# Mixture layers: the gate and up products of a tile as seven block products (Strassen) in place of eight, interleaved with the down products

## Chip, core and metric

The kernel runs on one core of a Trainium2 chip. The metric is the device time of one execution in microseconds (us); lower is better. The core has a matrix engine (PE, TensorE, with its weight loads shown as PEld), three engines for elementwise work (DVE or VectorE, ACT or ScalarE, POOL or GpSimd), and SyncE (SP), which here issues DMAs. Engines run their own instruction streams in order and wait for each other by semaphores.

## What is computed

Four layers, each an attention and a feed-forward, on 1024 tokens of width 256. The change touches the three mixture-of-experts feed-forwards (layers 1, 2 and 3). Cut to what matters, such a layer is

```
comb   = router weights per token and expert (top 2 of 8, 8 of 32, 4 of 16)
routed = sum over experts e of  comb[:, e] * ((silu(x @ w_gate[e]) * (x @ w_up[e])) @ w_down[e])
shared = (silu(x @ sw_gate) * (x @ sw_up)) @ sw_down        (layer 3: times a sigmoid gate)
x      = x + routed + shared
```

All experts are computed for all tokens, and the coefficient of a token that did not choose an expert is 0.

## The kernel before

**Tiles.** The hidden columns of the shared expert and of all experts are laid side by side and cut into tiles of 128: 14 tiles in layer 1, 34 in layer 2, 28 in layer 3, 76 in all (NT is a layer's number). A tile is one weight block of 128 hidden units against all 1024 tokens, which are held transposed (width on the partitions, two blocks k of 128; tokens in two halves c of 512).

**Three passes.** Every float32 operand of the big products is split into a rounded high part and the rest (type fp32r), and a product is three matmuls: high x high, high x low, low x high. So gate of one half is 2 blocks k times 3 passes, 6 matmuls of 128x128 by 128x512; up is 6 more; both halves make 24. The down product of a half is 2 output blocks times 3 passes, 6 matmuls, 12 for the tile. A tile is 36 matmuls.

**PSUM.** Eight banks of 128x512: p_g0, p_g1 (gate), p_u0, p_u1 (up) and the four p_y, in which the down products of all tiles add up.

**Work of the other engines on a tile.** ACT rounds the weights (`up_hi`, `down_hi`), takes the silu of the gate (`act_g`) and rounds the hidden values (`hid_hi`, by `high`). POOL makes the low parts of the weights (`up_lo`, `down_lo`) and multiplies by the coefficients (`hid`, by `weigh`). DVE multiplies silu by up (`gated`, by `gate`) and makes `hid_lo` (by `low`). SP loads weights and, for each routed tile, coefficient rows spread over partitions.

**Order.** There is no scheduler: each engine's order is written by hand in `mixture`, as a loop of two tiles (`Step` gives a loop-dependent tile number, `wait` a loop-dependent semaphore value). On PE it is gate and up of tile t+1, then down of tile t:

```
                        gate_up(Step(g, r + 2, 2))
                        down(Step(g, r + 1, 2))
```

On DVE it is `gate(t, 0)`, `gate(t, 1)`, `low(t, 0)`, `low(t, 1)`; on POOL `split_up(t + 1)`, `weigh(t, 0)`, `weigh(t, 1)`, `split_down(t + 1)`. Ahead of the loop each layer has a head: a layer norm, the transposes of x (`x_t`, split into `x_hi` and `x_lo`), the router on DVE, and tiles 0 and 1 written out, whose gate and up products PE runs while DVE ranks the experts.

## Time and profile before

| | before |
|---|---|
| median of 3 runs | 1289.76 us (1284.64 to 1299.0) |
| profiled execution: span, first to last instruction | 1274.6 us |
| PE busy | 1100.8 us, 86% |
| DVE busy | 674.0 us, 53% |
| ACT busy | 640.8 us, 50% |
| POOL busy | 524.5 us, 41% |
| granted TensorE clock, mean | 0.929 of full |

The times of single instructions below come from the one profiled execution, whose time is known as its span of 1274.6 us; the median of the runs is 15.2 us above that span. A row of the timeline reads: start, duration, engine, line, operation, output<-inputs, shapes, and in brackets how long the engine was idle before it and what released it. Matmuls of 512 columns start 0.23 us apart in a steady stretch while each is shown as 0.39 us long, since they overlap in the array; so the distance of starts, not the duration, is what a matmul costs.

### The profile page before, as it was taken

Reading aid. Unit: us, or ns where it says so; the run is one execution under the profiler, and the core shown is the slowest. Engines: PE = TensorE matmul, PEld = TensorE weight load, DVE = VectorE, ACT = ScalarE, POOL = GpSimd, SP = SyncE. Lnnn points to the kernel's source line nnn. Section 1 sums busy time; section 2 is a strip of 40 time slices with the busy share of each in tenths; the row PEclk is TensorE's granted clock in tenths of the full one; section 3 lists DMA queues with packets and bytes.
Section 4 is the critical chain, followed back from the end, with each engine's and each line's share of the span. In section 5 each row is a group of like instructions: output and inputs, shape, how many; then the busy total and the mean of one; then the engine's idle time right before and its main releaser. Section 6 shows DMA issues by size and latency. Waiting matters only on the chain. (4 is left out here: it accounts for less than half of the span.)

```text
span 1274.6 us, 19803 instructions
## 1 busy us (share of the span) xinstructions
PE 1100.8 (86%) x6973; PEld 799.6 (63%) x6974; DVE 674.0 (53%) x1388; ACT 640.8 (50%) x1016; POOL 524.5 (41%) x587
## 2 busy tenths in 40 slices
PE   4999622699699978998799999999967699999998
PEld 3545311444388865554578888888633478888887
DVE  5768578631653347785753333333577873333333
ACT  4557558489543334776334334443283454334443
POOL 5145700001246632123256656666401035666664
PEclk8789966899899998999799999999989889999999
DMA  5863130368223305431133353333100014333332
GB/s 162 244 191 125 52 115 1 84 181 193 77 96 115 112 29 160 147 116 46 53 120 115 115 177 110 111 111 106 37 9 1 1 40 145 115 113 107 111 110 69
DMA packets 65942, 131.40 MB, mean 103 GB/s; under 512 B 9307, under 2 KB 33051, under 8 KB 65366
## 3 DMA queue, kind: packets, MB, share of 16 engines
q1 hardware_dynamic: 62470, 123.10, 32.1%
q10 hardware_dynamic: 3120, 5.64, 1.4%
q0 software_dynamic: 288, 1.84, 0.4%
q8 instruction: 37, 0.61, 0.2%
q14 instruction: 27, 0.22, 0.1%
HBM read 114.51 MB, written 15.45 MB: 102 GB/s over the span
## 5 line engine op out<-in xcount | busy, mean ns | idle before, releaser
L1506 POOL TENSOR_TENSOR f_hid<-f_gated,f_coef 128x512 f32<-128x512 f32 x152 | 220.6, 1453 | 166.6 <-DVE f_gated L1538 157.0
L1538 DVE TENSOR_TENSOR f_gated<-f_act_g,f_p_u 128x512 f32<-128x512 f32 x152 | 104.2, 687 | 262.2 <-PE f_p_u L1322 245.6
L828 ACT ACTIVATE a_probs<-a_p_sc 128x1024 f32<-128x1024 f32 x192 | 188.9, 1020 | 27.4 <-PE a_p_sc L730 19.6
L1434 ACT ACTIVATE f_hid_hi<-f_hid 128x512 fp32r<-128x512 f32 x152 | 96.2, 633 | 203.8 <-POOL f_hid L1506 203.8
L959 DVE TENSOR_REDUCE a_maxes<-a_p_max 128x2 f32<-128x512 f32 x256 | 160.0, 682 | 41.6 <-PE a_p_max L697 41.4
L1542 DVE TENSOR_TENSOR f_hid_lo<-f_hid,f_hid_hi 128x512 fp32r<-128x512 f32 x152 | 112.6, 741 | 127.8 <-ACT f_hid_hi L1434 126.5
L1429 ACT ACTIVATE f_act_g<-f_p_g 128x512 f32<-128x512 f32 x152 | 90.4, 597 | 152.7 <-PE f_p_g L1322 148.5
L730 PE MATMUL a_p_sc<-a_q,a_k 75*128 75x256 bf16 (+1 forms) x768 | 117.8, 282 | 9.8 <-ACT a_probs L828 5.1
L1335 PE MATMUL f_p_y<-f_hid_hi,f_down_hi 128*128 128x512 f32 x292 | 114.0, 390 | 0.0
L1335 PE MATMUL f_p_y<-f_hid_hi,f_down_lo 128*128 128x512 f32 x292 | 113.7, 389 | 0.0
L1335 PE MATMUL f_p_y<-f_hid_lo,f_down_hi 128*128 128x512 f32 x292 | 113.7, 389 | 0.0
L750 PE MATMUL a_p_out<-a_probs,all_v 128*32 128x256 f32 x1536 | 110.7, 403 | 1.2 <-ACT a_probs L828 1.2
L1493 POOL TENSOR_TENSOR f_up_lo<-f_w,f_up_hi 128x512 fp32r<-128x512 f32 x76 | 97.6, 1285 | 31.4 <-DVE all_xn L183 20.1
L730 PEld LDWEIGHTS a_p_sc<-a_q,a_k 75*128 75x128 bf16 (+1 forms) x768 | 69.0, 100 | 56.4 <-issue 22.1
L697 PE MATMUL a_p_max<-a_k,a_q 72*128 72x256 bf16 x512 | 91.9, 293 | 12.3 <-DMA a_q<-q_parts 6.3
L1493 POOL TENSOR_TENSOR f_down_lo<-f_w,f_down_hi 128x256 fp32r<-128x256 f32 x76 | 70.5, 927 | 76.7 <-ACT f_down_hi L1424 76.7
L1322 PE MATMUL f_p_g<-f_x_hi,f_up_hi 128*128 128x512 f32 x304 | 95.8, 397 | 0.0
L1322 PE MATMUL f_p_g<-f_x_hi,f_up_lo 128*128 128x512 f32 x304 | 95.0, 394 | 0.0
L1322 PE MATMUL f_p_g<-f_x_lo,f_up_hi 128*128 128x512 f32 x304 | 94.9, 394 | 0.0
L1322 PE MATMUL f_p_u<-f_x_hi,f_up_hi 128*128 128x512 f32 x304 | 94.6, 392 | 0.0
L1322 PE MATMUL f_p_u<-f_x_lo,f_up_hi 128*128 128x512 f32 x304 | 93.9, 391 | 0.0
L1322 PE MATMUL f_p_u<-f_x_hi,f_up_lo 128*128 128x512 f32 x304 | 93.7, 389 | 0.0
(309 smaller groups left out, 1706.5 us busy)
## 6 DMA issues: line engine op xcount, KB each, us to landing
f_w<-in_w SPq DMA_DIRECT2D x76, 384.0 KB, 3.5
f_coef<-coef SPq DMA_DIRECT2D x49, 512.0 KB, 3.7
a_q<-q_parts SPq DMA_DIRECT2D x48, 288.0 KB
a_k<-k_plain SPq DMA_DIRECT2D x96, 96.0 KB
outs<-a_out SPq DMA_DIRECT2D x48, 128.0 KB, 1.7
a_whole<-outs SPq DMA_DIRECT2D x48, 128.0 KB, 2.6
q_parts<-a_q_part SPq DMA_DIRECT2D x48, 96.0 KB, 3.6
a_k<-k_unit SPq DMA_DIRECT2D x24, 192.0 KB
```

The lines of the kernel that those rows point to most:

```text
L697: last = nc.tensor.matmul(p_max[:, n % 3, t * D:(t + 1) * D], q_of(b, h, ROWS)[:, t * P:(t + 1) * P], k_of(b, h, ROWS), start=True, stop=True)
L730: last = nc.tensor.matmul(p_sc[pair % 2][:, h % 2, t * D:(t + 1) * D], k_of(b, h, K_ROWS)[:, t * P:(t + 1) * P], q_of(b, h, K_ROWS), start ...
L750: last = nc.tensor.matmul(p_out[32 * j:32 * j + 32, 0:D], m.v[:, b, at:at + 32], probs[b % 2][:, h, t, :], start=(quarter == 0), stop=(qua ...
L828: nc.scalar.activation(probs[b % 2][:, 2 * pair:2 * pair + 2, :, :].rearrange("p h t d -> p h (t d)"), p_sc[pair % 2][:], ACT.Exp, scale=s ...
L959: nc.vector.tensor_reduce(maxes[b % 3][:, :, h], p_max[:, n % 3, :].rearrange("p (t d) -> p t d", t=NK), axis=AX.X, op=ALU.max, negate=Tru ...
L1322: last = nc.tensor.matmul(p[:], w_[n][:, (2 * k + s) * P:(2 * k + s + 1) * P], x_[:, k, tok], start=(i == 0), stop=(i == len(passes) - 1))
L1335: last = nc.tensor.matmul(p_y[o][c][:], w_[n][:, o * P:(o + 1) * P], h_[n][c][:], start=False, stop=stop and i == len(passes) - 1, skip_gr ...
L1434: nc.scalar.activation(hid_hi[slot(t, 2)][c][:], hid[c][:], ACT.Copy).then_inc(hid_hi_done, 1)
L1493: nc.gpsimd.tensor_tensor(lo[slot(t, 2)][:], w[slot(t, 2)][:, cols], hi[slot(t, 2)][:], ALU.subtract).then_inc(lo_ready, 1)
L1506: nc.gpsimd.tensor_tensor(hid[c][:], gated[c][:], coef[slot(t, 2)][:, c * 512:(c + 1) * 512], ALU.mult).then_inc(hid_done, 1)
L1538: nc.vector.tensor_tensor(gated[c][:], act_g[c][:], p_u[c][:], ALU.mult).then_inc(gated_done, 1)
L1542: nc.vector.tensor_tensor(hid_lo[slot(t, 2)][c][:], hid[c][:], hid_hi[slot(t, 2)][c][:], ALU.subtract).then_inc(hid_lo_done, 1)
```

## The change

Gate and up of a tile are seen as one product of a 2x2 block matrix of weights (rows gate and up, columns the two width blocks k: A11, A12, A21, A22) with a 2x2 block matrix of tokens (rows k, columns the token halves: X11, X12, X21, X22). In place of eight block products (24 matmuls) it is made of seven, M1 to M7 (21 matmuls), in the Winograd form of Strassen's algorithm. What that adds:

- per tile, on DVE, `sum_weights`: four 128x128 sums of weight blocks, as one instruction of 3x128 and one of 2x128 columns, all in SBUF, for two tiles ahead;
- per tile, the split into high and low parts is 1024 columns wide in place of 512 (ACT `split_up`, POOL `split_up`);
- per tile, three copies of a PSUM bank to SBUF on ACT (`copy_m7`, `copy_m1`, `copy_u2`) and three adds of such a copy to a PSUM bank on DVE (`add_c11`, `add_c21`, `add_c22`), since an intermediate product goes into more than one result;
- once per layer, four sums of token blocks of 512 columns (`x_sum`) with their splits, ahead of the router's work on DVE and ahead of the first `weigh` on POOL;
- the four banks of gate and up become p_a0, p_a1 (by turns), p_b and p_cc, so one tile's products are no longer each in a bank of their own;
- weights come in two transfers per tile (up and down parts apart); the up part of tile t+2 is loaded once POOL has made `up_lo` of tile t.

Tiles 0 and 1 keep the eight products. From tile 2 on, all orders are new: the down products of tile t-1 lie between the block products of tile t, and `weigh`, `high` and `low` of the second half of tile t-1 lie in tile t. The diff, cut to its core (new semaphores, the heads and the second list of the last tile left out; `last_tile` is `tile` with m3 one step earlier):

```diff
@@ -1161,6 +1161,10 @@
 MIXTURES = {1: Mixture(8, 2, 176, 352), 2: Mixture(32, 8, 128, 256), 3: Mixture(16, 4, 176, 704)}
 GROUPS, TOP_GROUPS, ROUTED_SCALE = 8, 4, 2.5
 UP = NK * 2 * P
+SUMS = 2 * UP
+GATE_AT, UP_AT = (0, 3), (1, 2)
+A11, A21, A22, A12, S3, R2, S1, S4, V = range(9)
+X11, X12, X21, X22, T1, P2, T3, P4 = range(8)
...
-        x_hi = st.sb("x_hi", [P, NK, T], F32R)
-        x_lo = st.sb("x_lo", [P, NK, T], F32R)
+        x_hi = st.sb("x_hi", [P, 4 * NK, 512], F32R)
+        x_lo = st.sb("x_lo", [P, 4 * NK, 512], F32R)
...
+        x_sum = m.xn[:].rearrange("p (b i) d -> p b (i d)", b=4)
+        m1_copy, m7_copy, u2_copy = x_t[:, 0, 0:512], x_t[:, 0, 512:1024], x_t[:, 1, 0:512]
...
-        w = [st.sb(f"w{n}", [P, UP + D]) for n in range(2)]
-        up_hi = [st.sb(f"up_hi{n}", [P, UP], F32R) for n in range(2)]
-        up_lo = [st.sb(f"up_lo{n}", [P, UP], F32R) for n in range(2)]
+        w_up = [st.sb(f"w_up{n}", [P, SUMS + P]) for n in range(2)]
+        w_down = [st.sb(f"w_down{n}", [P, D]) for n in range(2)]
+        up_hi = [st.sb(f"up_hi{n}", [P, SUMS], F32R) for n in range(2)]
+        up_lo = [st.sb(f"up_lo{n}", [P, SUMS], F32R) for n in range(2)]
...
+        p_a, p_b, p_cc = p_g, p_u[1], p_u[0]
...
+                def load_up(t):
+                    if t >= 2:
+                        sp.wait_ge(up_lo_ready, t - 1)
+                    sp.dma_start(w_up[t % 2][:, 0:UP], a[f"w{layer}"][t, :, 0:UP]).then_inc(up_loaded[t % 2], 16)
+                def load_down(t):
+                    if t >= 2:
+                        sp.wait_ge(down_lo_ready, t - 1)
+                    sp.dma_start(w_down[t % 2][:], a[f"w{layer}"][t, :, UP:UP + D]).then_inc(down_loaded[t % 2], 16)
...
-                    if t > 2:
-                        wait(sp, down_lo_ready, t, 1, -1)
-                        sp.dma_start(w[t % 2][:], a[f"w{layer}"][t, :, :]).then_inc(w_loaded[t % 2], 16)
+                    load_down(t)
...
+                    if t + 2 < NT:
+                        load_up(t + 2)
...
+                def product(t, bank, w_at, x_at, start, done):
                     n = slot(t, 2)
+                    for i, (w_, x_) in enumerate(((up_hi, x_hi), (up_hi, x_lo), (up_lo, x_hi))):
+                        last = nc.tensor.matmul(bank[:], w_[n][:, w_at * P:(w_at + 1) * P], x_[:, x_at, :],
+                                                start=start and i == 0, stop=(i == 2), skip_group_check=True)
+                    last.then_inc(done, 1)
+                def m7(t):
+                    wait(pe, up_lo_ready, t, 1, 1)
+                    wait(pe, gated_done, t, 2, -1)
+                    product(t, p_cc, S3, T3, True, m7_done)
+                def m1(t):
+                    wait(pe, silu_done, t, 2, -2)
+                    product(t, p_a[slot(t, 2)], A11, X11, True, m1_done)
+                def m2(t):
+                    wait(pe, gated_done, t, 2, 0)
+                    product(t, p_b, A12, X21, True, m2_done)
+                def m6(t):
+                    wait(pe, m1_copied, t, 1, -1)
+                    product(t, p_a[slot(t, 2)], R2, P2, False, m6_done)
+                def m4(t):
+                    wait(pe, m7_copied, t, 1, -1)
+                    product(t, p_cc, A22, P4, False, m4_done)
+                def m5(t):
+                    wait(pe, u2_copied, t, 1, -1)
+                    product(t, p_a[slot(t, 2)], S1, T1, False, m5_done)
+                def m3(t):
+                    wait(pe, c22_done, t, 1, -1)
+                    product(t, p_a[slot(t, 2)], S4, X22, False, m3_done)
...
+                def tile(t):
+                    m7(t)
+                    m1(t)
+                    down(t + (-1), 0, 0)
+                    m2(t)
+                    m6(t)
+                    m4(t)
+                    down(t + (-1), 0, 1)
+                    m5(t)
+                    down(t + (-1), 1, 0)
+                    down(t + (-1), 1, 1)
+                    m3(t)
...
-                        gate_up(Step(g, r + 2, 2))
-                        down(Step(g, r + 1, 2))
-                down(NT - 1, stop=True)
+                        tile(Step(g, r + 2, 2))
+                tile(NT - 2)
+                last_tile(NT - 1)
+                for c in range(2):
...
+                def split_up(t, width=SUMS):
+                    if width == SUMS:
+                        wait(act, summed, t, 1, -1)
+                    else:
+                        act.wait_ge(up_loaded[t], 16)
+                    nc.scalar.activation(up_hi[slot(t, 2)][:, 0:width], w_up[slot(t, 2)][:, 0:width],
                                          ACT.Copy).then_inc(up_hi_ready, 1)
...
+                def silu_first(t):
+                    wait(act, c11_done, t, 1, -1)
+                    nc.scalar.activation(act_g[0][:], p_b[:], ACT.Silu).then_inc(silu_done, 1)
+                def silu_second(t):
+                    wait(act, m3_done, t, 1, -1)
+                    nc.scalar.activation(act_g[1][:], p_a[slot(t, 2)][:], ACT.Silu, scale=-1.0).then_inc(silu_done, 1)
+                def copy_m1(t):
+                    wait(act, m1_done, t, 1, -1)
+                    nc.scalar.activation(m1_copy, p_a[slot(t, 2)][:], ACT.Copy).then_inc(m1_copied, 1)
+                def copy_m7(t):
+                    wait(act, m7_done, t, 1, -1)
+                    nc.scalar.activation(m7_copy, p_cc[:], ACT.Copy).then_inc(m7_copied, 1)
+                def copy_u2(t):
+                    wait(act, m6_done, t, 1, -1)
+                    nc.scalar.activation(u2_copy, p_a[slot(t, 2)][:], ACT.Copy).then_inc(u2_copied, 1)
...
+                    copy_m7(t)
+                    copy_m1(t)
                     if more:
                         split_up(t + 1)
-                    silu(t, 0)
-                    silu(t, 1)
+                    high(t + (-1), 1)
+                    copy_u2(t)
+                    silu_first(t)
+                    split_down(t)
                     high(t, 0)
-                    high(t, 1)
-                    if more:
-                        split_down(t + 1)
+                    silu_second(t)
...
+                def split_up(t, width=SUMS):
+                    wait(pool, up_hi_ready, t, 1, 1)
+                    nc.gpsimd.tensor_tensor(up_lo[slot(t, 2)][:, 0:width], w_up[slot(t, 2)][:, 0:width],
+                                            up_hi[slot(t, 2)][:, 0:width], ALU.subtract).then_inc(up_lo_ready, 1)
...
+                    weigh(t + (-1), 1)
                     if more:
                         split_up(t + 1)
                     weigh(t, 0)
-                    weigh(t, 1)
-                    if more:
-                        split_down(t + 1)
+                    split_down(t)
...
+                def sum_weights(t):
+                    tile_w = w_up[slot(t, 2)]
+                    dve.wait_ge(up_loaded[slot(t, 2)], uses(t, 2) * 16 + 16)
+                    nc.vector.tensor_tensor(blocks(tile_w, S3, 2, 3), blocks(tile_w, A11, 1, 3),
+                                            blocks(tile_w, A21, 1, 3), ALU.subtract).then_inc(differed, 1)
+                    wait(dve, differed, t, 1, -1)
+                    nc.vector.tensor_tensor(blocks(tile_w, R2, 2, 2), blocks(tile_w, S3, 0, 2),
+                                            blocks(tile_w, A22, V - A22, 2), ALU.add).then_inc(summed, 1)
+                def add_c11(t):
+                    wait(dve, m2_done, t, 1, -1)
+                    wait(dve, m1_copied, t, 1, -1)
+                    nc.vector.tensor_tensor(p_b[:], p_b[:], m1_copy, ALU.add).then_inc(c11_done, 1)
+                def add_c21(t):
+                    wait(dve, m4_done, t, 1, -1)
+                    wait(dve, u2_copied, t, 1, -1)
+                    nc.vector.tensor_tensor(p_cc[:], p_cc[:], u2_copy, ALU.add).then_inc(c21_done, 1)
+                def add_c22(t):
+                    wait(dve, m5_done, t, 1, -1)
+                    wait(dve, m7_copied, t, 1, -1)
+                    nc.vector.tensor_tensor(p_b[:], p_a[slot(t, 2)][:], m7_copy, ALU.add).then_inc(c22_done, 1)
+                def gate_first(t):
+                    wait(dve, silu_done, t, 2, 1)
+                    wait(dve, c21_done, t, 1, -1)
+                    nc.vector.tensor_tensor(gated[0][:], act_g[0][:], p_cc[:], ALU.mult).then_inc(gated_done, 1)
+                def gate_second(t):
+                    wait(dve, silu_done, t, 2, 2)
+                    wait(dve, c22_done, t, 1, -1)
+                    nc.vector.scalar_tensor_tensor(gated[1][:], p_b[:], -1.0, act_g[1][:], ALU.mult,
+                                                   ALU.mult).then_inc(gated_done, 1)
...
+                def tile(t, more=True):
+                    if more:
+                        sum_weights(t + 2)
+                    add_c11(t)
+                    low(t + (-1), 1)
+                    add_c21(t)
+                    gate_first(t)
+                    add_c22(t)
                     low(t, 0)
-                    low(t, 1)
+                    gate_second(t)
...
+                x11, x12, x21, x22 = [x_t[:, k, c * 512:(c + 1) * 512] for k in range(NK) for c in range(2)]
+                v.scalar_tensor_tensor(x_sum[:, 0, :], x11, -1.0, x12, ALU.mult, ALU.subtract).then_inc(x_sum_ready, 1)
+                dve.wait_ge(x_sum_ready, 1)
+                v.tensor_tensor(x_sum[:, 1, :], x_sum[:, 0, :], x22, ALU.subtract).then_inc(x_sum_ready, 1)
+                v.tensor_tensor(x_sum[:, 2, :], x22, x12, ALU.add).then_inc(x_sum_ready, 1)
+                dve.wait_ge(x_sum_ready, 2)
+                v.tensor_tensor(x_sum[:, 3, :], x21, x_sum[:, 1, :], ALU.subtract).then_inc(x_sum_ready, 1)
+                sum_weights(2)
...
-    gu = gu.reshape(2, NK, P, mx.tiles, P).transpose(3, 2, 1, 0, 4).reshape(mx.tiles, P, UP)
+    gu = gu.reshape(2, NK, P, mx.tiles, P)
+    gu = np.stack([gu[0, 0], gu[1, 0], gu[1, 1], gu[0, 1]], 0).transpose(2, 1, 0, 3).reshape(mx.tiles, P, UP)
```

DVE, the loop body for one tile in layer 1, before (f1_gated0 is half 0, f1_hid_lo10 the low part of slot 1, half 0):

```order
L1538 TENSOR_TENSOR f1_gated0<-f1_act_g0,f1_p_u0 128x512
L104 REGISTER_ALU
L1538 TENSOR_TENSOR f1_gated1<-f1_act_g1,f1_p_u1 128x512
L1542 TENSOR_TENSOR f1_hid_lo10<-f1_hid0,f1_hid_hi10 128x512
L1542 TENSOR_TENSOR f1_hid_lo11<-f1_hid1,f1_hid_hi11 128x512
```

The same engine and place now (f1_w_up0 holds the weight blocks and their sums, f1_x_t the three copies):

```order
L1698 TENSOR_TENSOR f1_w_up0<-f1_w_up0 128x3x128
L104 ISA
L1701 TENSOR_TENSOR f1_w_up0<-f1_w_up0 128x2x128
L104 REGISTER_ALU
L1707 TENSOR_TENSOR f1_p_u1<-f1_p_u1,f1_x_t 128x512
L104 ISA
L1732 TENSOR_TENSOR f1_hid_lo11<-f1_hid1,f1_hid_hi11 128x512
L1712 TENSOR_TENSOR f1_p_u0<-f1_p_u0,f1_x_t 128x512
L104 REGISTER_ALU
L1722 TENSOR_TENSOR f1_gated0<-f1_act_g0,f1_p_u0 128x512
L1717 TENSOR_TENSOR f1_p_u1<-f1_p_g0,f1_x_t 128x512
L1732 TENSOR_TENSOR f1_hid_lo00<-f1_hid0,f1_hid_hi00 128x512
```

Four instructions per tile have become nine (the ninth, gate_second, follows the last row). The two sums come first, and the low part of the other half of the tile before stands between two adds on which later products wait.

POOL, one tile of the loop in layer 1, before:

```order
L1493 TENSOR_TENSOR f1_up_lo0<-f1_w0,f1_up_hi0 128x512
L1504 ISA
L104 ISA
L1506 TENSOR_TENSOR f1_hid0<-f1_gated0,f1_coef1 128x512
L104 REGISTER_ALU
L1506 TENSOR_TENSOR f1_hid1<-f1_gated1,f1_coef1 128x512
L1493 TENSOR_TENSOR f1_down_lo0<-f1_w0,f1_down_hi0 128x256
```

And now:

```order
L1656 TENSOR_TENSOR f1_hid1<-f1_gated1,f1_coef1 128x512
L104 ISA
L1638 TENSOR_TENSOR f1_up_lo1<-f1_w_up1,f1_up_hi1 128x1024
L1654 ISA
L104 REGISTER_ALU
L1656 TENSOR_TENSOR f1_hid0<-f1_gated0,f1_coef0 128x512
L104 REGISTER_ALU
L1643 TENSOR_TENSOR f1_down_lo0<-f1_w_down0,f1_down_hi0 128x256
```

The low part of the up weights is twice as wide and stands between the two halves' multiplications by coefficients, right behind the second half of the tile before.

## Rows read from the trace of the kernel before

**Rows 1.** The page: first line, part 1, and the first of part 4's lines:

```profile
span 1274.6 us, 19803 instructions
PE 1100.8 (86%) x6973; PEld 799.6 (63%) x6974; DVE 674.0 (53%) x1388; ACT 640.8 (50%) x1016; POOL 524.5 (41%) x587
PE f_p_g L1322 6%; PE f_p_u L1322 6%; PE f_p_y L1335 6%; PE f_p_y L1371 0%; DVE f_ln_stats L152 0%; PE f_p_y L1348 0%; DVE all_xn L183 0%; DVE all_x L1634 0%; PE f_p_y L1381 0%; DVE f_x_t L1562 0%; PE f_p_y L1392 0%; DVE f_y_t L1631 0%; DVE f_ln_mv L159 0%; DVEq L1269 0%; ACT f_ln_root L139 0%
```

**Rows 2.** Windows: stretch, length, each engine's busy time, granted clock, DMA share, GB/s:

```profile
1100.00:1116.32 16.32, 16.32 (x74) 13.52 (x73) 5.34 (x9) 6.58 (x12) 10.31 (x8) 1.00 0.37 112
627.60:630.00 2.40, 2.40 (x8) 1.92 (x8) 1.50 (x5) 1.67 (x2) 0.00 (x0) 0.50 0.01 3
```

**Rows 3.** Timeline of one tile of layer 3, in the loop:

```profile
1101.98 0.62 PE L1322 MATMUL f_p_g<-f_x_hi,f_up_hi 128*128 128x512 f32 x2
...
1105.61 0.62 PE L1322 MATMUL f_p_g<-f_x_hi,f_up_lo 128*128 128x512 f32 x2
1105.74 1.29 POOL L1506 TENSOR_TENSOR f_hid<-f_gated,f_coef 128x512 f32<-128x512 f32 x1 [0.53 <-DVE f_gated L1538]
...
1106.27 0.60 ACT L1429 ACTIVATE f_act_g<-f_p_g 128x512 f32<-128x512 f32 x1 [2.12 <-PE f_p_g L1322]
...
1107.07 0.63 ACT L1434 ACTIVATE f_hid_hi<-f_hid 128x512 fp32r<-128x512 f32 x1 [0.20 <-POOL f_hid L1506]
...
1107.69 0.69 DVE L1538 TENSOR_TENSOR f_gated<-f_act_g,f_p_u 128x512 f32<-128x512 f32 x1 [2.03 <-PE f_p_u L1322]
...
1108.30 0.68 DVE L1542 TENSOR_TENSOR f_hid_lo<-f_hid,f_hid_hi 128x512 fp32r<-128x512 f32 x1
...
1108.46 1.68 POOL L1506 TENSOR_TENSOR f_hid<-f_gated,f_coef 128x512 f32<-128x512 f32 x1 [1.43 <-DVE f_gated L1538]
...
1110.14 0.62 PE L1322 MATMUL f_p_g<-f_x_hi,f_up_hi 128*128 128x512 f32 x2
```

**Rows 4.** Timeline, DVE and POOL at once, layer 1:

```profile
360.23 1.29 POOL L1506 TENSOR_TENSOR f_hid<-f_gated,f_coef 128x512 f32<-128x512 f32 x1 [1.39 <-DVE f_gated L1538]
360.33 1.73 DVE L1542 TENSOR_TENSOR f_hid_lo<-f_hid,f_hid_hi 128x512 fp32r<-128x512 f32 x1
...
363.46 1.29 POOL L1493 TENSOR_TENSOR f_up_lo<-f_w,f_up_hi 128x512 fp32r<-128x512 f32 x1
...
364.02 0.67 DVE L1538 TENSOR_TENSOR f_gated<-f_act_g,f_p_u 128x512 f32<-128x512 f32 x1
```

**Rows 5.** Timeline, layer 2: POOL's two rows, then DVE's:

```profile
639.34 0.74 POOL L1493 TENSOR_TENSOR f_down_lo<-f_w,f_down_hi 128x256 fp32r<-128x256 f32 x1 [1.05 <-ACT f_down_hi L1424]
640.04 1.46 POOL L1493 TENSOR_TENSOR f_up_lo<-f_w,f_up_hi 128x512 fp32r<-128x512 f32 x1
...
639.46 0.91 DVE L1612 TENSOR_TENSOR f_picked<-f_picked,f_scores 128x256 f32<-128x256 f32 x1
```

**Rows 6.** Groups of instructions: count, busy us, mean ns, idle before:

```profile
L1424 ACT ACTIVATE f_down_hi<-f_w 128x256 fp32r<-128x256 f32 x76 | 30.5, 401 | 0.0
L2271 DVE TENSOR_TENSOR c_s<-c_s,c_top 128x1024 f32<-128x1024 f32 x8 | 9.8, 1225 | 0.3
L1855 ACT ACTIVATE b_junk<-b_h 128x1024 f32<-128x1024 f32 x8 | 8.5, 1060 | 0.1
```

**Rows 7.** Timeline, head of layer 2:

```profile
628.66 1.06 PE L1322 MATMUL f_p_g<-f_x_lo,f_up_hi 128*128 128x512 f32 x2
629.52 1.05 PE L1322 MATMUL f_p_g<-f_x_hi,f_up_lo 128*128 128x512 f32 x2
...
642.18 1.06 PE L1392 MATMUL f_p_y<-all_ident,f_by_token 128*33 128x128 f32 x8 [1.40 <-DVE f_by_token L1619]
```

**Rows 8.** Timeline, end of layer 3:

```profile
1265.88 0.69 DVE L1542 TENSOR_TENSOR f_hid_lo<-f_hid,f_hid_hi 128x512 fp32r<-128x512 f32 x1 [1.85 <-ACT f_hid_hi L1434]
...
1266.62 0.50 PE L1335 MATMUL f_p_y<-f_hid_hi,f_down_hi 128*128 128x512 f32 x1
```

**Rows 9.** DMA issues: KB each, median us to landing:

```profile
f_w<-in_w SPq DMA_DIRECT2D x76, 384.0 KB, 3.5
```

184 lines of the change are left out of this document (119 added, 65 removed).

## The prediction

> **What bounds the kernel now.** I read the page's first part and the chain that ended last, then a stretch inside a mixture loop by windows, then one tile of the timeline, and at last the places where DVE and POOL work at once. PE is busy 86% of the span and heads the chain, with gate, up and down at about equal shares [rows 1]. In a 16.32 us stretch of layer 3 PE is busy all of it at clock 1.00, while POOL is busy 10.31 us, ACT 6.58 and DVE 5.34 [rows 2]. The first gate matmul of one tile starts at 1101.98 and that of the next at 1110.14 [rows 3]: a period of 8.16 us for 36 matmuls, 0.2267 us each, with nothing idle. So the loop is bound by the number of matmuls, and everything else is hidden as long as it keeps up. The loop rows repeat in all three layers; of the 76 tiles, NT - 3 periods per layer lie between the start of tile 2 and that of the last tile: 11 + 31 + 25 = 67.
>
> **What is taken away.** 3 of 36 matmuls per tile: 3 x 0.2267 = 0.68 us. If PE stays the bound, the period is 33 x 0.2267 = 7.48 us, and 67 periods give 45.6 us.
>
> **What is added, and whether it is hidden.** By busy time all engines still fit. ACT: three 512-wide copies at 0.60 (taken as the silu's row), the split at 1.06 (the 1024-wide row) in place of 0.6, the rest as before (two silus at 0.60, two highs at 0.63, 0.40 for down): 5.7 us [rows 3, 6]. DVE: gates and adds read one operand from PSUM, 5 x 0.69; two lows at 0.68; the sums of 3x128 and 2x128 columns at 0.56 and 0.43, from the 0.68 of 512 and the 1.225 of 1024 columns: 5.8 us [rows 3, 6]. POOL: 512 columns take 1.29 us, 256 take 0.74, so 1024 take about 2.39; with two weighs and the down part 5.7 us [rows 3, 5]. On that count alone PE would be late for nothing.
>
> But DVE and POOL shut each other out. At 360.33 DVE starts a low part 0.10 us behind a POOL multiplication that ends at 361.52; DVE ends at 362.06, after 1.73 us in place of 0.68 [rows 4]: it got through only 0.54 us after POOL was done. The other way round, POOL's weigh at 1108.46 meets a low part that ends at 1108.98 and ends itself at 1110.14: 1.68 us, 1.16 of them after the low part [rows 3]. An instruction of DVE that reads two operands in SBUF and one of POOL thus take turns. A gate, which reads one from PSUM, doesn't: it takes 0.67 us in the middle of POOL's work [rows 4]. And who asks first gets in first: between two POOL instructions back to back, at 640.08, a waiting DVE instruction of 256 columns gets in, ends 0.29 us later, and the second POOL one takes 1.46 [rows 5]. Before, this costs nothing, since DVE waits most of the time.
>
> The change puts five kinds of such work in one narrow place. Time in which the pair is held, per tile: POOL 1.16 + 1.16 for the weighs, 0.60 for the down part (0.74 less the 0.13 that POOL needs ahead of it), and for the 1024-wide low part 1.16 + 2 x 0.55 = 2.26; DVE 0.54 + 0.54 for the lows, 0.42 and 0.29 for the sums. Sum 6.97 of 7.48 us. The pair would have to be held without a break, but what it does is chained.
>
> **The chain of one tile,** from the start of gate_second of tile t-1 (0) to that of tile t, each step by the rows above: DVE issues the sum of three blocks 0.61 later (the distance from 1107.69 to 1108.30 [rows 3]), asks 0.14 later, and holds for 0.42: 1.17. The weigh of tile t-1's second half asked meanwhile, holds 1.16: 2.33. The sum of two blocks has asked by then, holds 0.29: 2.62. POOL's 1024-wide low part is next in its queue and holds 2.26: 4.88. All this while DVE has done c11 and stands at low(t-1, 1), whose input (ACT's high) has been ready since about 3.0 but which asked after POOL: it ends 0.54 later, 5.42. Behind it in DVE's queue are add_c21 (issued 0.08 before that end, 0.69, and 0.03 to the wait for its own result) to 6.06 and gate_first to 6.75. Then POOL weighs half 0 (0.05 + 1.29) to 8.09, ACT rounds it (0.04 + 0.63) to 8.76, DVE starts low(t, 0) at 8.80 and gate_second 0.61 later: 9.41 us per tile. PE finds low(t-1, 1) missing for the down products of half 1 (some 1.2 us idle), and c22 missing for m3 (some 0.6). 7.48 + 1.9 is the same 9.4.
>
> So each period grows by 9.41 - 8.16 = 1.25 us: 67 x 1.25 = +84 us, where PE alone would have given -46.
>
> Bounds of this term. The one row that doesn't exist is the 1024-wide POOL instruction. If it let DVE in halfway, as two of 512 would by [rows 5], DVE's low part would come 1.1 us earlier and the loop close at 8.3 us: +9 us. If the sum of three blocks loses its turn against the weigh (it asks only 0.12 us earlier), it and the second sum come behind longer POOL work and the loop closes at about 10.0: +123 us. The adds, which write PSUM, have no row either; between 0.6 and 1.0 us they move the period to 9.3 and 9.7. I take 9.41, since every hold that is shown lasted to the end of its instruction. The Trainium skill (page SBUF — State Buffer, section Who interferes with whom) calls this an exclusive lock: a VectorE instruction with two SBUF inputs and a GpSimd one that reads SBUF block each other for the full instruction. Taken to the letter it would also hold for the 0.13 and 0.14 us at the start of each, which the rows show outside the lock; the sum by it would be some 0.5 us more per tile.
>
> **Heads and ends.** Four sums of 512 columns and the first weight sums stand ahead of the router's chain on DVE: 4 x 0.61 + 1.0 = 3.5 us, more where POOL is in the way. In layer 2 PE already waits 1.40 us for that chain [rows 7], so all of it is late there, in the other two I count 3 to 4: +4 us each, +12 (between 0 and 24). At the end of a layer PE waited little before: the last low part ended at 1266.57 and PE went on at 1266.62 with 12 matmuls before it to hide it [rows 8]. Now gate_second of the last tile follows m3, and only one down block and half 0 lie beside silu 0.60, gate 0.69, weigh 1.29, high 0.63, low 0.69: +2.5 each, +7.
>
> **Cover that holds.** Weights of tile t+2 are asked for when up_lo of tile t is done, some 5 us before DVE's sums need them; such a load took 3.5 us at 1.5 times the size [rows 9]. If it took over 5 us, the sums, and with them all of DVE, would wait for it.
>
> **The sum.** 84 + 12 + 7 = +103 on the span of 1274.6: 1378. The median of the runs is 15.2 above the span before; kept, that is 1289.8 + 103 = 1393 us.
>
> **Rivals.**
> 1. *PE stays the bound* (faster). The pair of DVE and POOL finds its gaps in another order than I have laid out, and the period is 7.48. For it: all busy times fit. Against: [rows 3, 4, 5], and 6.97 of 7.48 us held. -46 + 12 + 7 = -27: 1263 us. It decides if the long POOL instruction doesn't shut DVE out.
> 2. *The long low part shuts DVE out only in part.* Period 8.3 to 8.9: +9 to +50, with heads and ends 1318 to 1359 us.
> 3. *Sum and weigh change places.* Period 10.0: 1289.8 + 123 + 19 = 1432 us. They ask 0.12 us apart, so it could also come and go.
> 4. *The clock falls.* In the head of layer 2 the granted clock is 0.50 [rows 2] and pairs of matmuls start 0.86 us apart in place of 0.45 [rows 7], 1.2 against 2.4 GHz. PE would then need 33 x 0.43 = 14.2 us per tile. With idle times of at most 1.2 us in a tile I think it stays at 1.00; if a tenth of the loop ran so, that is some 7 tiles times 4.8 us, +34 us on the forecast.
> 5. *It doesn't do what it says*: 21 matmuls in place of 24 stand in the order, so this is excluded.
>
> **Chances.** Forecast (1365 to 1420) 0.66; rival 1 0.12, of which 0.01 within 1%; rival 2 0.11; rival 3 0.07; rival 4 0.04. Less than 1% can't be told from no change by such measurements. Faster by over 1% 0.12, within 1% 0.03, slower 0.85. The range leaves out rival 1 and the lower half of rival 2 and takes in nearly all else: 1330 to 1435.
>
> **What the profile after would show.** Starts of the second silu 9.4 us apart in all three loops. In rows of DVE: f_hid_lo at a mean of 1.3 us or more, half of them over 2 us and each of these ending half a microsecond after the 1024-wide f_up_lo, which takes 2.4 to 2.6; the two-block sum at 1.4 and not 0.43. DVE busy about 89% of a stretch, PE's idle time in front of f_p_y, released by f_hid_lo, and in front of m3, released by DVE's add. Granted clock 1.00. I am wrong if f_hid_lo keeps its 0.69 us beside the long POOL instruction, or if PE is idle for a reason other than these two.

## The result: 8.8% slower

The changed kernel takes 1401.74 us (median of 4 runs, 1399.15 to 1406.09), the kernel before 1289.11 (4 runs, 1284.64 to 1299.0): ratio 1.0877, 95% interval 1.0822 to 1.0932. Forecast were 1393 us and a range of 1330 to 1435.

The page of the changed kernel, its first line, part 1 and the first two lines of part 4 (the chain that ended last); [rows 1] answers to it:

```profile
span 1404.3 us, 20549 instructions
...
PE 1125.2 (80%) x6763; PEld 755.1 (54%) x6764; DVE 1032.7 (74%) x1750; ACT 773.2 (55%) x1238; POOL 604.0 (43%) x599
...
issue 9%; POOL 9%; DVE 2%; DMA 1%; ACT 1%; POOLq 0%; PE 0%; DVEq 0%; SPq 0%
POOL f_up_lo L1638 4%; POOL f_hid L1656 3%; POOL f_down_lo L1643 1%; POOL f_x_lo L1649 0%; DMA coef<-f_coef_t 0%; DMA f_coef<-coef 0%; ACT f_hid_hi L1567 0%; DVE f_x_lo L1762 0%; DVE f_ln_stats L152 0%; DVE all_xn L183 0%; DVE f_x_t L1757 0%; PE f_p_y L1413 0%; DVE all_x L1844 0%; POOLq L104 0%; DVE f_p_u L1712 0%
```

PE has 210 matmuls fewer and yet 24 us more of busy time. About 9 us of that lie in the three loops, where its rows grow when it restarts after a pause; 8 lie in the heads, where the lower granted clock lasts longer in layers 1 and 2, and 8 ahead of the first mixture, in code that is the same. The chain is now led by POOL, with the long low part of the up weights first in it. One window of one period in layer 3 (columns as in [rows 2]):

```profile
1198.00:1207.46 9.46, 8.24 (x34) 5.91 (x33) 7.87 (x10) 5.07 (x9) 6.06 (x5) 1.00 0.30 97
```

No engine is busy all of it (DVE 83%, PE 87%), and the granted clock is 1.00: this loop is bound by an order of turns, not by an engine's work. Behind the loops' entries the starts of the second `gate` lie 9.45 to 9.48 us apart in all three layers, where before a period was 8.16 [rows 3]. That shows in the groups of instructions (count, busy us, mean ns, idle before and its releaser):

```profile
L1732 DVE TENSOR_TENSOR f_hid_lo<-f_hid,f_hid_hi 128x512 fp32r<-128x512 f32 x152 | 206.9, 1362 | 118.5 <-ACT f_hid_hi L1567 118.3
...
L1638 POOL TENSOR_TENSOR f_up_lo<-f_w_up,f_up_hi 128x1024 fp32r<-128x1024 f32 (+1 forms) x76 | 186.3, 2451 | 27.2 <-DVE all_xn L183 20.1
...
L1413 PE MATMUL f_p_y<-f_hid_hi,f_down_hi 128*128 128x512 f32 x292 | 128.3, 440 | 71.4 <-DVE f_hid_lo L1732 71.4
L1372 PE MATMUL f_p_g<-f_x_hi,f_up_hi 128*128 128x512 f32 x280 | 117.6, 420 | 23.5 <-DVE f_p_u L1717 23.5
...
L1701 DVE TENSOR_TENSOR f_w_up<-f_w_up 128x256 f32<-128x256 f32 x70 | 93.5, 1336 | 2.4
```

`f_hid_lo` takes 1.36 us on average and not 0.69, the two-block sum 1.34 and not 0.43. Nearly all of PE's idle time in the loops stands in front of the two products named: 71.4 us ahead of the down products, released by `f_hid_lo`, and 23.5 us ahead of m3, released by DVE's add. The timeline of that tile:

```profile
1202.65 0.69 DVE L1717 TENSOR_TENSOR f_p_u<-f_p_g,f_x_t 128x512 f32<-128x512 f32 x1
...
1203.40 0.50 PE L1372 MATMUL f_p_g<-f_x_hi,f_up_hi 128*128 128x512 f32 x1 [0.34 <-DVE f_p_u L1717]
...
1205.40 0.69 DVE L1727 SCALAR_TENSOR_TENSOR f_gated<-f_p_u,f_act_g 128x512 f32<-128x512 f32 x1
...
1206.00 0.55 DVE L1698 TENSOR_TENSOR f_w_up<-f_w_up 128x384 f32<-128x384 f32 x1
1206.17 1.54 POOL L1656 TENSOR_TENSOR f_hid<-f_gated,f_coef 128x512 f32<-128x512 f32 x1 [1.37 <-DVE f_gated L1727]
...
1206.59 1.41 DVE L1701 TENSOR_TENSOR f_w_up<-f_w_up 128x256 f32<-128x256 f32 x1
...
1207.67 2.58 POOL L1638 TENSOR_TENSOR f_up_lo<-f_w_up,f_up_hi 128x1024 fp32r<-128x1024 f32 x1
...
1207.92 0.69 DVE L1707 TENSOR_TENSOR f_p_u<-f_p_u,f_x_t 128x512 f32<-128x512 f32 x1
...
1208.52 2.29 DVE L1732 TENSOR_TENSOR f_hid_lo<-f_hid,f_hid_hi 128x512 fp32r<-128x512 f32 x1
...
1210.73 0.69 DVE L1712 TENSOR_TENSOR f_p_u<-f_p_u,f_x_t 128x512 f32<-128x512 f32 x1
...
1210.86 0.50 PE L1413 MATMUL f_p_y<-f_hid_hi,f_down_hi 128*128 128x512 f32 x1 [0.86 <-DVE f_hid_lo L1732]
```

The low part that starts at 1208.52 ends at 1210.81, 0.56 us after POOL's wide instruction (1210.25), as behind the short one in [rows 4]; each of the 64 low parts of over 2 us in the trace ends 0.54 or 0.55 us after one (by unrounded times). The add at 1207.92, with an operand in PSUM, takes its 0.69 in the middle of it.

**Where the time went.** Of each profiled execution I took the stretch from a layer's first low part of the up weights to its last add on x: before 125.5, 292.1 and 241.6 us in layers 1 to 3, after 148.5, 343.7 and 288.7, +122 in all.
- Heads, to the start of tile 2: before 21.4, 24.6, 23.2, after 26.0, 31.6, 28.1: +16.5. Four of the runs below (e2, e3, e7, e9) leave these heads' work as it is and take 30.4 in layer 2; in the changed kernel the granted clock fell to 0.50 for 3.4 us at the end of that head, which is about the difference.
- Periods: 67 x 1.30 = +87.
- Entry to the loop: the second and third periods are longer than 9.46 by 1.6, 2.9 and 7.3 in the three layers: +11.7. Part of it is the clock (see e9).
- Ends: what is left of the difference, about +6.

Outside the mixtures the span is 7.9 us longer, 6.9 of it ahead of the first one, in code that the change leaves alone; this point also moved between the other kernels (347 to 359 us), so I don't count it to the change.

### The profile page after: what moved, and what is told of

Its sections match the earlier page's. It is cut to its first block and busy times, and to the rows that moved or that the text cites. A ratio compares the mean times of both kernels' runs of the same rounds, so it can differ in the third digit from the quotient of the medians.

```text
span 1404.3 us, 20549 instructions
## 1 busy us (share of the span) xinstructions
PE 1125.2 (80%) x6763; PEld 755.1 (54%) x6764; DVE 1032.7 (74%) x1750; ACT 773.2 (55%) x1238; POOL 604.0 (43%) x599
## 5 line engine op out<-in xcount | busy, mean ns | idle before, releaser
L1732 DVE TENSOR_TENSOR f_hid_lo<-f_hid,f_hid_hi 128x512 fp32r<-128x512 f32 x152 | 206.9, 1362 | 118.5 <-ACT f_hid_hi L1567 118.3
L1638 POOL TENSOR_TENSOR f_up_lo<-f_w_up,f_up_hi 128x1024 fp32r<-128x1024 f32 (+1 forms) x76 | 186.3, 2451 | 27.2 <-DVE all_xn L183 20.1
L1413 PE MATMUL f_p_y<-f_hid_hi,f_down_hi 128*128 128x512 f32 x292 | 128.3, 440 | 71.4 <-DVE f_hid_lo L1732 71.4
L1372 PE MATMUL f_p_g<-f_x_hi,f_up_hi 128*128 128x512 f32 x280 | 117.6, 420 | 23.5 <-DVE f_p_u L1717 23.5
L1413 PEld LDWEIGHTS f_p_y<-f_hid_hi,f_down_hi 128*128 128x128 f32 x292 | 55.0, 188 | 126.3 <-DVE f_hid_lo L1732 108.6
L1372 PE MATMUL f_p_g<-f_x_lo,f_up_hi 128*128 128x512 f32 x280 | 110.2, 394 | 0.0
L1372 PE MATMUL f_p_g<-f_x_hi,f_up_lo 128*128 128x512 f32 x280 | 110.1, 393 | 0.0
L969 DVE RECIPROCAL a_inv<-a_whole 128x64 f32<-128x64 f32 (+1 forms) x48 | 45.5, 947 | 81.0 <-DMA a_whole<-outs 81.0
L1701 DVE TENSOR_TENSOR f_w_up<-f_w_up 128x256 f32<-128x256 f32 x70 | 93.5, 1336 | 2.4
L1372 PEld LDWEIGHTS f_p_g<-f_x_hi,f_up_hi 128*128 128x128 f32 x280 | 52.8, 189 | 63.2 <-DVE f_p_u L1717 53.1
```

The costliest lines, as they stand in the source:

```text
L1372: last = nc.tensor.matmul(bank[:], w_[n][:, w_at * P:(w_at + 1) * P], x_[:, x_at, :], start=start and i == 0, stop=(i == 2), skip_group_ch ...
L1413: last = nc.tensor.matmul(p_y[o][c][:], w_[n][:, o * P:(o + 1) * P], h_[n][c][:], start=False, stop=stop and i == len(passes) - 1, skip_gr ...
L1638: nc.gpsimd.tensor_tensor(up_lo[slot(t, 2)][:, 0:width], w_up[slot(t, 2)][:, 0:width], up_hi[slot(t, 2)][:, 0:width], ALU.subtract).then_i ...
L1701: nc.vector.tensor_tensor(blocks(tile_w, R2, 2, 2), blocks(tile_w, S3, 0, 2), blocks(tile_w, A22, V - A22, 2), ALU.add).then_inc(summed, 1)
L1732: nc.vector.tensor_tensor(hid_lo[slot(t, 2)][c][:], hid[c][:], hid_hi[slot(t, 2)][c][:], ALU.subtract).then_inc(hid_lo_done, 1)
```

## The experiments

The first four ran with 13 runs of the kernel before (median 1290.84), the next four with 7 (1292.01), the last with 11 (1289.68). "Period" is the distance between starts of the second gate.

| run | median us (range) | ratio to before, 95% | period |
|---|---|---|---|
| changed kernel | 1401.74 (1399.15–1406.09) | 1.0877 (1.0822–1.0932) | 9.46 |
| e1_two_halves | 1334.73 (1331.21–1335.84) | 1.0344 (1.0289–1.0399) | 8.36 |
| e2_low_later | 1364.91 (1360.95–1366.83) | 1.0565 (1.0506–1.0623) | 8.73 |
| e3_no_sums | 1373.83 (1372.2–1379.53) | 1.0640 (1.0583–1.0697) | 9.04 |
| e4_pool_writes_only | 1299.99 (1292.14–1306.22) | 1.0090 (1.0053–1.0126) | 7.86 |
| e5_before_21 | 1238.57 (1234.01–1241.21) | 0.9603 (0.9573–0.9633) | 7.48 |
| e6_no_input_sums | 1395.98 (1392.29–1400.72) | 1.0828 (1.0791–1.0865) | 9.46 |
| e7_reorder | 1310.69 (1309.66–1314.05) | 1.0161 (1.0127–1.0195) | 7.96 |
| e8_reorder_head | 1308.07 (1304.12–1309.52) | 1.0139 (1.0108–1.0169) | 7.96 |
| e9_load_early | 1398.38 (1396.91–1400.88) | 1.0839 (1.0803–1.0875) | 9.46 |

**e1: the wide low part as two instructions.** Same elements, one gap more.

```diff
-                    nc.gpsimd.tensor_tensor(up_lo[...][:, 0:width], w_up[...][:, 0:width], up_hi[...][:, 0:width], ALU.subtract)
+                    for lo in range(0, width, UP):
+                        nc.gpsimd.tensor_tensor(up_lo[...][:, lo:lo + UP], w_up[...][:, lo:lo + UP], up_hi[...][:, lo:lo + UP], ALU.subtract)
```

> The changed kernel with POOL's 1024-wide low part of the up weights issued as two instructions of 512 columns; nothing else differs, POOL's busy time is the same. Theory A (DVE instructions with two SBUF operands and POOL's take turns, first come first served, each to the end of its instruction): DVE's low part of the second half gets in between the two halves, some 1.1 us earlier, and the period of a tile falls from the 9.46 us shown to 8.3; 67 periods, 1402 - 78 = 1324 us. f_hid_lo's longest instances fall from 2.3 to about 1.2 us. Theory B (POOL or DVE is simply full, or its work is too long for the chain): no change, 9.46 us and 1402.

Timeline, layer 3, POOL's row and then DVE's:

```profile
1203.85 3.19 POOL L1639 TENSOR_TENSOR f_up_lo<-f_w_up,f_up_hi 128x512 fp32r<-128x512 f32 x2
...
1204.70 1.18 DVE L1735 TENSOR_TENSOR f_hid_lo<-f_hid,f_hid_hi 128x512 fp32r<-128x512 f32 x1
```

DVE gets in between the halves and is through at 1205.88, while POOL works until 1207.04 and takes 0.7 us longer in all than one instruction of 1024 columns (2.45). The period falls by 1.10 us, which is 74 us over 67 periods; the medians differ by 67, where 78 was expected. All that although POOL does more. So not the amount of work counts but how long one instruction keeps the other side out.

**e2: the waiting instruction moved.** DVE's low part of half 1 stands behind `gate_first`; nothing else changes.

```diff
-                    low(t + (-1), 1)
                     add_c21(t)
                     gate_first(t)
+                    low(t + (-1), 1)
```

> The changed kernel with one line moved in DVE's order: low(t-1, 1) stands behind gate_first(t) in place of ahead of add_c21(t). The same instructions, the long POOL instruction as it is. Theory A: DVE's add_c21 and gate_first no longer stand behind an instruction that is shut out; the low part is still late for the down products. Period 8.6 us, 1402 - 58 = 1344 us. Theory B (DVE's or POOL's amount of work): 9.46 and 1402, since the amount is unchanged. A third, that PE's missing low part alone sets the period: no gain or a loss, since the low part comes later.

All 152 low parts take 0.69 us, so POOL's wide instruction now blocks none. The same instructions in another order shorten the period by 0.73 of the 1.30 us that it had grown: more than half of the loss was in what stood queued behind the blocked one. In the medians that is 37 us where I expected 58: the period is 8.73 and not 8.6 (9 us), the entries of the loops are 4 us longer than in the changed kernel, and the rest is open.

**e3: without the weight sums** (from tile 4 on the sums of tiles 2 and 3 are used again, so the products are of other weights; ACT's rounding, whose change is left out here, waits for the load in place of the sums).

```diff
-                    if more:
-                        sum_weights(t + 2)
                     add_c11(t)
```

> The changed kernel without the weight sums inside the loop: they are made for tiles 2 and 3 only, later tiles multiply by those old sums. It leaves out 1 us of DVE work per tile and 0.71 us in which the pair of DVE and POOL is held; the split stays 1024 wide. Theory A: period 8.9 us, 1402 - 38 = 1364 us, the two holds of 0.42 and 0.29 gone from the chain but the long low part still in it. Theory C (the sums are what breaks it): the period falls to 7.5 to 7.8, 1402 - 120 = 1280 us.

The sums cost 0.4 us per period; the 2.2 us low part stays, and with it most of the loss. The period of 9.04 is a little over the 8.9 expected, and so is the median, by 10 us.

**e4: POOL writes in place of reading** (128 of 1024 columns are real, the rest of the low part is set to zero, and a memset of a spare buffer fills up the time, to 2.0 us in place of 2.45).

```diff
+                    part = P if width == SUMS else width
+                    nc.gpsimd.tensor_tensor(up_lo[...][:, 0:part], w_up[...][:, 0:part], up_hi[...][:, 0:part], ALU.subtract)
+                    if width == SUMS:
+                        nc.gpsimd.memset(scratch[...][:], 0.0)
+                        nc.gpsimd.memset(up_lo[...][:, P:].bitcast(F32), 0.0)
```

> The changed kernel with POOL's long low part replaced by work that hardly reads: 128 columns of it are still made, the rest is a memset of the other 896 columns and a memset of a spare 600-column tile, about 1.9 us in all against 2.4. The low parts of the weights are left out but for one block. Theory A (shut out while POOL reads SBUF): period 7.8 us, 1402 - 111 = 1290 us, f_hid_lo back at 0.7 us nearly everywhere. Theory B (the time that POOL's queue needs for it): only the 0.5 us that it is shorter, 8.95 us and 1367. If a memset shuts DVE out as well, the same as B.

Timeline, layer 3, POOL's rows and then DVE's:

```profile
1204.87 0.66 POOL L1640 TENSOR_TENSOR f_up_lo<-f_w_up,f_up_hi 128x128 fp32r<-128x128 f32 x1
1205.46 0.60 POOL L1643 MEMSET f_scratch<- 128x600 bf16 x1
1206.00 0.85 POOL L1644 MEMSET f_up_lo<- 128x896 f32 x1
...
1205.72 0.68 DVE L1738 TENSOR_TENSOR f_hid_lo<-f_hid,f_hid_hi 128x512 fp32r<-128x512 f32 x1
```

DVE's low part runs its 0.68 us right through POOL's two memsets, across the gap between them; so it isn't the splitting into three instructions that lets it in. The period drops to 7.86, below the 8.16 of the kernel before, yet the whole stays 9 us above it: the heads, entries and ends cost some 29 us by themselves (67 x 0.30 = 20 gained, 9 lost).

**e5: three matmuls fewer and nothing added.** In the kernel before, one of six matmuls is left out in three of a tile's four gate and up groups (so a low-part pass of one block is missing in each).

```diff
+                            if isinstance(t, Step) and 2 * c + s < 3:
+                                passes = passes[:-1]
```

> The kernel before, in which from tile 2 on three of the 24 gate and up matmuls of a tile are left out (one of the six in three of the four groups), so 33 per tile; all else of a tile is as before. It measures by itself what three matmuls fewer are worth while the other engines keep up. If PE's count of matmuls is the bound of the kernel before, the period falls from 8.16 to 33 x 0.2267 = 7.48 us and the median by 67 x 0.68 = 46 us, to about 1245 us. If another limit stands close behind (the weights' DMA, POOL with 5.1 us per tile, or a clock that falls as PE's waits grow), the period stays at 7.7 or more and the median at 1260 or more.

The period is 7.48 to the hundredth, and PE is busy all of a 14.96 us stretch at clock 1.00. The time falls by 53 us, more than the 46 expected, and only 2 us of the difference have a reason in the count (70 tiles lose matmuls, not 67: 70 x 0.68 = 48). So what the change was to save is there to be had, and no other limit stands close behind.

**e6: without the input sums** (the products read the plain blocks of x in their place).

> The changed kernel without the four sums of token blocks in the head of each layer and without their rounding on ACT and low parts on POOL; the products that read them read the four plain blocks instead, so the values differ, and the number of matmuls stays. It isolates what these sums cost a head. In layer 2's head the four sums take 2.5 us of DVE ahead of the router, and four router instructions that meet POOL's low parts of the sums take 1.50, 1.53, 1.26 and 1.27 us in place of 0.43, 0.42, 0.29 and 0.29, 4.1 us more. If the head is late for that, tile 2 of layer 2 starts 5 us earlier and those of layers 1 and 3 some 3 to 4, so the median falls by about 12, to 1390 us, with the period unchanged at 9.46. If the heads are late for another reason (the wider first split, the loads in two parts), the median falls by less than 4 us.

The head of layer 2, of the changed kernel first, POOL's row and then DVE's:

```profile
659.21 5.44 POOL L1649 TENSOR_TENSOR f_x_lo<-all_xn,f_x_hi 128x512 fp32r<-128x512 f32 x4 [5.35 <-ACT f_x_hi L1617]
...
659.24 1.53 DVE L1701 TENSOR_TENSOR f_w_up<-f_w_up 128x256 f32<-128x256 f32 x1
660.70 1.50 DVE L1793 TENSOR_TENSOR f_ranked<-f_scores,f_bias 128x256 f32<-128x256 f32 x1
662.23 1.26 DVE L1796 TENSOR_TENSOR f_pair_hi<-f_ranked 128x128 f32<-128x128 f32 x1
663.52 1.27 DVE L1797 TENSOR_TENSOR f_pair_lo<-f_ranked 128x128 f32<-128x128 f32 x1
```

and of this run:

```profile
654.86 0.42 DVE L1697 TENSOR_TENSOR f_w_up<-f_w_up 128x256 f32<-128x256 f32 x1
655.20 0.42 DVE L1783 TENSOR_TENSOR f_ranked<-f_scores,f_bias 128x256 f32<-128x256 f32 x1
655.65 0.29 DVE L1786 TENSOR_TENSOR f_pair_hi<-f_ranked 128x128 f32<-128x128 f32 x1
```

Four POOL instructions held up four of DVE's, one each: a weight sum of tile 2 and, behind it, three of the router's. The head of layer 2 is 6.6 us shorter, of which 1.2 is the clock named above, but those of layers 1 and 3 only 1.0 and 1.3: 8.9 of the 16.5 us, and 5.8 in the medians, where I expected 12. Of the other 7.6 us no run shows the cause; the weight sums of tiles 2 and 3 and the first wide split are the candidates.

**e7: all of the change, in another order.** I laid a period out step by step with the durations and holds of the rows, and moved instructions until none waited long.

```diff
-                    m7(t); m1(t); down(t-1, 0, 0); m2(t); m6(t); m4(t); down(t-1, 0, 1); m5(t); down(t-1, 1, 0); down(t-1, 1, 1); m3(t)
+                    m1(t); m7(t); m2(t); m6(t); m4(t); down(t-1, 0, 0); m5(t); down(t-1, 0, 1); down(t-1, 1, 1); m3(t); down(t-1, 1, 0)
# ACT
-                    copy_m7(t); copy_m1(t); split_up(t + 1); high(t-1, 1); copy_u2(t); silu_first(t); ...
+                    split_up(t + 1); copy_m1(t); copy_m7(t); copy_u2(t); silu_first(t); high(t-1, 1); ...
# DVE as in e2
```

(Calls stand on one line here. Left out are the waits that move with them, so that M1 and not M7 waits for `up_lo`, two waits ahead of the loops, and the last tile, which now takes the same list.)

> The changed kernel with all its work, in another order, found by laying out a period step by step with the durations and holds of the rows: PE runs M1 before M7, all of M1, M7, M2, M6, M4 ahead of the first down product, and the down products of half 1 around M3; ACT rounds the next tile's weights first; DVE puts the low part of half 1 behind gate_first. The layout gives a period of 7.90 us, and 9.40 for the order as changed. If DVE and POOL take turns by order of asking and only the order makes the 9.46 us, the period is 7.9 and the median 1291 - 67 x 0.26 + 30 for heads and ends as in the other runs = 1304 us. If the amount of work on the pair makes the period, it stays above 9 us and the median above 1370. A layout that is off by a lost turn would show 8.3 to 8.6, 1330 to 1350 us.

Timeline, layer 3, POOL's rows and then DVE's:

```profile
1202.81 1.53 POOL L1647 TENSOR_TENSOR f_hid<-f_gated,f_coef 128x512 f32<-128x512 f32 x1 [1.37 <-DVE f_gated L1718]
1204.31 2.59 POOL L1629 TENSOR_TENSOR f_up_lo<-f_w_up,f_up_hi 128x1024 fp32r<-128x1024 f32 x1
...
1203.22 1.40 DVE L1692 TENSOR_TENSOR f_w_up<-f_w_up 128x256 f32<-128x256 f32 x1
1204.55 0.69 DVE L1698 TENSOR_TENSOR f_p_u<-f_p_u,f_x_t 128x512 f32<-128x512 f32 x1
1205.48 0.70 DVE L1703 TENSOR_TENSOR f_p_u<-f_p_u,f_x_t 128x512 f32<-128x512 f32 x1 [0.24 <-PE f_p_u L1372]
1206.28 0.69 DVE L1713 TENSOR_TENSOR f_gated<-f_act_g,f_p_u 128x512 f32<-128x512 f32 x1
1206.88 0.68 DVE L1723 TENSOR_TENSOR f_hid_lo<-f_hid,f_hid_hi 128x512 fp32r<-128x512 f32 x1
```

Beside POOL's wide instruction DVE now has two adds and a gate, which all have an operand in PSUM and all keep their 0.69 us; the low part asks when POOL is about done. The period is 7.96 (7.90 laid out), 91 us come back with not one instruction less, and the loop is faster than before. In sum it is still 1.6% slower (1.3 to 2.0%), which is clear of the noise but under 2%: 67 x 0.20 = 13 us gained in the periods, some 32 lost around them. The time is 7 us above what I expected, 4 of them since the period is 7.96 and not 7.90.

**e8: e7 with other heads.** DVE makes the low parts of the input sums, the weight sums of tile 2 stand behind the second gate, and the up weights of tile 4 are asked for early (as in e9).

> As the reordered kernel, and the heads changed: the low parts of the input sums are made by DVE (0.61 us each) and not by POOL, with their high parts ahead of the scores on ACT; the weight sums of tile 2 move from ahead of the router's chain to behind its second gate; and the up weights of tile 4 are asked for ahead of the store of the coefficients, since in the changed kernel DVE waited for them 3.3 us in layer 2, and PE 2.1 us behind that. Expected against the reordered kernel: the wait for the weights gone, 2 us per layer, and the router 1.2 us earlier in layer 2, about as much in the others: together -7 to -10 us, 1295 us. If the early wait for weights was covered by other waits, only -3 us.

The wait for weights is gone: from tile 2 to the end layer 3 takes 7.2 us less than in e7 (218.1 against 225.3). But the heads are no shorter (26.5, 32.1, 28.7 against 26.0, 30.4, 28.1). The router's result reaches PE 0.4 us earlier in layer 2, where 1.2 was expected, and no earlier in the other two; at the end of layer 2's head the granted clock is 0.50 for 6.8 us, as it isn't in e7 at that place. And in the middle of layer 2, where SP also issues loads for the next attention, one period took 11.25 us and the next 8.38. DVE's rows there, and POOL's:

```profile
788.65 1.19 DVE L1689 TENSOR_TENSOR f_w_up<-f_w_up 128x384 f32<-128x384 f32 x1 [0.60 <-DMA f_w_up<-in_w]
789.87 2.51 DVE L1692 TENSOR_TENSOR f_w_up<-f_w_up 128x256 f32<-128x256 f32 x1
...
788.13 1.30 POOL L1648 TENSOR_TENSOR f_hid<-f_gated,f_coef 128x512 f32<-128x512 f32 x1 [1.37 <-DVE f_gated L1718]
789.38 2.72 POOL L1630 TENSOR_TENSOR f_up_lo<-f_w_up,f_up_hi 128x1024 fp32r<-128x1024 f32 x1
```

The weights came 0.60 us late; so POOL's multiplication asked before the first sum, and POOL's wide instruction before the second. That is rival 3, sum and weigh changing places, in one tile. The two periods are 3.7 us longer for 0.6 us of lateness, but not by the turns alone: PE paused for 2.25 us, and its next eight matmuls ran at the lower clock, 0.43 us apart, some 1.6 us in all. The window shows it (columns as in [rows 2]):

```profile
795.10:798.40 3.30, 3.30 (x8) 2.62 (x9) 1.18 (x2) 1.05 (x2) 1.71 (x2) 0.50 0.12 36
```

The median is 1308 us where I expected 1295, and its interval overlaps that of e7. No version of the change here beats the kernel before.

**e9: the missed term by itself.** One transfer moved ahead of the store of the coefficients.

```diff
                 load_up(3)
+                load_up(4)
                 sp.wait_ge(coef_t_ready, 2)
...
-                    if t + 2 < NT:
+                    if 4 < t + 2 < NT:
                         load_up(t + 2)
```

> The changed kernel with one transfer moved: the up weights of tile 4 are asked for ahead of the store of the router's coefficients, not behind it and behind the coefficient rows of tile 2. In the changed kernel DVE's first weight sum of the loop waited for these weights 7.6 us in layer 3 and 3.4 in layer 1, and PE 5.4 us behind it in layer 3. If that wait is what makes the second period of layer 3 16.05 us and not 9.46, that period falls to 10 or 11, the second periods of layers 1 and 2 (11.0 and 12.2) by less, since part of DVE's wait there lies beside its wait for other things, and the median falls by 5 to 9 us, to 1395. If the store and the coefficient rows then come later and hold POOL's first multiplications up instead, the time doesn't move.

The entry of layer 3's loop in the changed kernel, DVE's row and PE's:

```profile
1150.28 0.56 DVE L1698 TENSOR_TENSOR f_w_up<-f_w_up 128x384 f32<-128x384 f32 x1 [7.63 <-DMA f_w_up<-in_w]
...
1152.55 0.79 PE L1413 MATMUL f_p_y<-f_hid_hi,f_down_hi 128*128 128x512 f32 x1 [5.40 <-DVE f_hid_lo L1732]
```

and in this run:

```profile
1143.39 1.64 DVE L1699 TENSOR_TENSOR f_w_up<-f_w_up 128x384 f32<-128x384 f32 x1
1145.07 2.51 DVE L1702 TENSOR_TENSOR f_w_up<-f_w_up 128x256 f32<-128x256 f32 x1
...
1148.83 0.50 PE L1414 MATMUL f_p_y<-f_hid_hi,f_down_hi 128*128 128x512 f32 x1 [0.86 <-DVE f_hid_lo L1733]
```

The second periods are 10.66 in all three layers (11.02, 12.23 and 16.05 in the changed kernel); the three mixtures together are 8.3 us shorter. Part of that is the clock. Behind the pause of 5.40 us the changed kernel's PE ran 13 matmuls 0.43 us apart, some 2.6 us more than at the full clock:

```profile
1151.30:1158.10 6.80, 5.55 (x13) 4.39 (x14) 4.48 (x8) 2.16 (x5) 1.98 (x2) 0.50 0.09 29
```

In the second period of layer 2 the same happened for 3.4 us. In this run, without the wait, the granted clock stays 1.00 through the loops. What remains, 1.2 us each, is the two sums: in the first round they ask behind POOL's multiplication and its wide low part, and take 1.64 and 2.51. In the medians it is 3.4 us, less than the 5 to 9 expected and within what two sets of runs tell apart; the rows carry this point, not the times.

## Why the prediction was right

The mechanism and the place were right; by its steps:

- *PE saves 0.68 us per tile*: e5 shows 7.48 us and no other limit near.
- *Two SBUF operands on DVE and POOL take turns, to the end of the instruction*: e1 and e2 show it from two sides, one by giving DVE a gap and one by letting DVE ask later, and e4 takes the reading away and the block is gone. e3, in turn, leaves the sums out and the block stays. Turns are given in the order of asking: the sum of three blocks always won against the weigh, so rival 3 came in no period of the changed kernel's steady loop; it is what happens in e8 when a sum comes late, and in the first round of e9.
- *The chain of one tile, 9.41 us*: 9.46 measured, and the steps fit as well: from gate_second (1205.40) the blocked low part was laid out to end at 5.42, and ends at 5.41. The range's ends for it were priced well too: two halves give 8.36 where 8.3 was laid out.
- *PE idle 1.2 and 0.6 us*: shown as 0.86 and 0.34, but by starts (1209.61 to 1210.86, 1202.67 to 1203.40, less 0.23) it is 1.02 and 0.50, and the next matmul starts 0.1 late each time.
- *DVE busy 89%*: the durations of its rows sum to 8.39 us of 9.46, which is 89%, but each row overlaps the next by some 0.08 us, and a window counts that once: 7.87, 83%.
- *Heads +12*: +16.5, by layer 4.6, 7.0 and 4.9 against 4 each. In layer 2 the router isn't late by the 3.5 us of added work alone; POOL's low parts of the input sums meet a weight sum and three router instructions (e6: 5.4 us for sums and block, and 1.2 of the clock). I had the rule in hand and wrote "more where POOL is in the way" without pricing it.
- *Ends +7*: about 6.
- *The weights' load is covered*: this step failed. I set the 3.5 us of a load against 5 us of lead in the loop. At the loop's entry the load stands in SP's queue behind the store of the coefficients and the coefficient rows of tile 2. In layer 3 it was issued at 1144.46, 1.8 us after DVE had begun to wait for it, and DVE went on 5.8 us later, where such a load took 2.6 in the median; the coefficient rows had been issued 0.5 us before it. So it was late twice over, and the pause cost clock besides: the entries are +11.7 us, of which e9 gives 8.1 back.
- *15.2 us above the span*: that was no overhead. Each run's time lies 1.7 to 2.4 us above its own span; the profiled execution of before was shorter than all 31 timed runs of that kernel whose spans are known (1276.1 to 1295.5 us). These go with the mean granted clock: the shortest of the 31 shows 0.927, the longest 0.912, the profiled execution 0.929. It did no harm to the forecast, since a difference was added to a median. But it makes the differences disagree: 130 us between the two spans, 113 between the medians; the profiled execution lies 12.7 us under the median of before and that of the changed kernel 4.3 over its own. The forecast of +103 lies below both. The parts of the sum were 19 us short of the +122 that the traces show in the mixtures; that the median came within 9 us of 1393 owes something to this scatter, so to luck.

Rival 1 fell: the period is 9.46 and not 7.48. Rival 2 is what e1 makes of the change. Rival 4 fell for the steady part of the loops, where the clock was 1.00, but not at their entries: I argued from idle times of at most 1.2 us in a tile, and behind the 5.40 us at layer 3's entry the clock did fall.
